# A selective-scan kernel: states in half blocks, sums on TensorE's column halves, residuals on TensorE and ScalarE

## Chip, cores and metric

One Trainium2 chip, one core of it. The metric is the device time of the whole program in microseconds (us); the time before is the median of 3 runs.

## What is computed

64 sequences of 205 rows (128 made by a token mixer out of `x`, 77 of text) and 1024 channels go through an attention-like state-space layer and a feed-forward layer, each with a layer norm ahead and a residual. The part that matters here:

```python
A = -jnp.exp(A_log)                                  # 1024 channels x 16 states
xp = jnp.einsum('bld,rd->blr', x, x_proj_w)          # x is the layer norm of h
dt_in, B, C = xp[..., :32], xp[..., 32:48], xp[..., 48:]
dt = jax.nn.softplus(jnp.einsum('blr,dr->bld', dt_in, dt_proj_w) + dt_proj_b)
dA = jnp.exp(dt[..., None] * A)
dBx = dt[..., None] * B[:, :, None, :] * x[..., None]
def step(h, inp):
    dA_t, dBx_t, C_t = inp
    h = dA_t * h + dBx_t
    y = jnp.einsum('bdn,bn->bd', h, C_t)             # sum over the 16 states
    return (h, y)
y = ys + D * x
h = h + y                                            # first residual
h = h + ffn(layernorm(h))                            # second residual, dequantized weights
```

## The kernel before, in words

Constants, the token mixer and the dequantized weights take the first 480 us or so; `scan_pass` takes the rest. It is a software pipeline over the 64 sequences. In entry `u` the scan of sequence `u` runs, while sequence `u+1` is prepared (layer norm 1, transpose, x and dt projections), `u-1` gets its first residual, layer norm 2 and the feed-forward product, and `u-2` its second residual. Two entries are one body of a hardware loop.

The scan of a sequence has 32 chunks. A chunk is one block of 128 channels (on the partitions) and 4 of the 16 states (205 columns each, 820 in all). For each chunk:

- ScalarE writes `decay = exp(dt * A)` into one of two PSUM buffers, 4 activations of 205 columns (L1003). It waits for the buffer's last reader, two chunks back.
- GpSimd writes `B * u` into one of 8 ring buffers (L1107), where `u = dt * x` was made by it earlier (L1128).
- VectorE scans the 820 columns (L1162). A large dt at column 0 (`reset` on ScalarE, L1085) makes the decay there 0, so that a state does not run into the next.
- The product with `C` is made by VectorE (L1168, chunks in the tuple `ON_DVE`, 19 of 32) or by GpSimd (L1113, the other 13, three chunks later).
- TensorE adds the states up: an identity of 128x128 times each 205-column slice, accumulated in the PSUM bank `y_ps` over 4 chunks (L899), after one product with `diag(D)` (L893). It stands `LAG` = 3 chunks behind. ScalarE copies the block out (`blk`, L1041).

All other work stands in tables written out by hand, one per engine: `PE_PLAN`, `ACT_PLAN`, `DVE_PLAN` and `POOL_PLAN` say behind which chunk each stage stands. Both residuals come as TensorE transposes into one of two exchange banks (`xch`, L915 and L946) that VectorE adds to the rows in `h1` (`add`, L1183; `finish`, L1197), 8 additions a sequence. `mean` for layer norm 2 then reads the 1024 columns again with an accumulator (L1019). The exchange banks go round in the order of `X_ORDER`. SyncE issues all transfers in program order in its `entry`: keep the rows, load the next, spread B and C over 128 partitions (`spread`, L840 and L842), write the result, load the rows for the residual.

```python
for n in range(CN):
    last = nc.tensor.matmul(y_ps, ident[:, :], ring[:, c % RING, n * LEN:(n + 1) * LEN],
                            start=False, stop=(c % 4 == 3 and n == CN - 1))
last.then_inc(sum_done, 1)
```

## Time and profile before

| | |
|---|---|
| median of 3 runs | 6199.3 us (6199.27 to 6200.41) |
| the profiled execution, its own time | 6200.29 us |
| its span | 6198.4 us |
| TensorE's granted clock, mean | 0.979 |
| busy: PE, DVE, POOL, ACT | 93%, 92%, 92%, 83% of the span |
| sequences | 64, one every 87.5 us |

The span is the time from the first to the last instruction. Busy times are unions: two instructions of an engine that overlap at their edges count once, so a mean duration times a count comes to more than the busy time. Consecutive small instructions of ScalarE and VectorE overlap by some 0.06 to 0.1 us, and the distance from start to start is what one of them really takes of its engine. A float32 product is two passes on TensorE, with two records; a transpose is one.

### The profile page before, as it was taken

Reading aid. Unit: us, or ns where it says so; the run is one execution under the profiler, and the core shown is the slowest. Engines: PE = TensorE matmul, PEld = TensorE weight load, DVE = VectorE, ACT = ScalarE, POOL = GpSimd, SP = SyncE. Lnnn points to the kernel's source line nnn. Section 1 sums busy time; section 2 is a strip of 40 time slices with the busy share of each in tenths; the row PEclk is TensorE's granted clock in tenths of the full one; section 3 lists DMA queues with packets and bytes.
Section 4 is the critical chain, followed back from the end, with each engine's and each line's share of the span. In section 5 each row is a group of like instructions: output and inputs, shape, how many; then the busy total and the mean of one; then the engine's idle time right before and its main releaser. Section 6 shows DMA issues by size and latency. Waiting matters only on the chain. (4 is left out here: it accounts for less than half of the span.)

```text
span 6198.4 us, 111922 instructions
## 1 busy us (share of the span) xinstructions
PE 5792.6 (93%) x35091; PEld 5385.1 (87%) x35091; DVE 5699.7 (92%) x4564; ACT 5122.6 (83%) x12831; POOL 5709.3 (92%) x3484
## 2 busy tenths in 40 slices
PE   4686999999999999999999999999999999999998
PEld 3555899999999999999999999999999999999997
DVE  8766999999999999999999999999999999999996
ACT  5716888888888888888888888888888888888885
POOL 4627999999999999999999999999999999999995
PEclk9887999999999999999999999999999999999999
DMA  4701222122212221222122212221222212221220
GB/s 94 161 2 66 83 88 71 67 83 88 74 64 83 88 78 66 78 88 83 61 78 88 88 56 80 86 88 61 77 83 88 72 67 83 88 78 61 83 83 34
DMA packets 115881, 478.49 MB, mean 77 GB/s; under 512 B 17441, under 2 KB 52401, under 8 KB 107122
## 3 DMA queue, kind: packets, MB, share of 16 engines
q1 hardware_dynamic: 115314, 471.10, 22.2%
q8 instruction: 335, 5.49, 0.4%
q14 instruction: 232, 1.90, 0.1%
HBM read 327.82 MB, written 143.24 MB: 76 GB/s over the span
## 5 line engine op out<-in xcount | busy, mean ns | idle before, releaser
L1107 POOL TENSOR_TENSOR s_ring<-s_bc,s_u_t 128x820 f32<-128x820 f32 x2048 | 3617.5, 1788 | 4.2 <-DMA s_bc<-rows_bc 4.2
L1003 ACT ACTIVATE s_decay<-s_dt_t,a_neg 128x205 f32<-128x205 f32 x8192 | 3047.2, 420 | 418.4 <-DVE s_ring L1168 347.5
L899 PE MATMUL s_y_ps<-s_ring,ident 128*128 128x205 f32 x16384 | 3140.6, 341 | 113.5 <-issue 61.5
L899 PEld LDWEIGHTS s_y_ps<-s_ring,ident 128*128 128x128 f32 x16384 | 2864.1, 191 | 204.9 <-POOL s_ring L1113 112.8
L1162 DVE TENSOR_TENSOR_SCAN s_decay<-s_decay,s_ring 128x820 f32<-128x820 f32 x1216 | 2265.0, 1863 | 193.6 <-ACT s_decay L1003 180.0
L1113 POOL TENSOR_TENSOR s_ring<-s_ring,s_bc 128x820 f32<-128x820 f32 x832 | 1605.4, 1930 | 77.7 <-DVE s_ring L1162 77.6
L1162 DVE TENSOR_TENSOR_SCAN s_ring<-s_decay,s_ring 128x820 f32<-128x820 f32 x832 | 1543.3, 1855 | 40.9 <-ACT s_decay L1003 40.9
L932 PE MATMUL s_xch<-s_x_t,w_low 128*128 128x205 f32 x8192 | 1523.6, 338 | 0.6 <-ACT s_x_t L1046 0.2
L932 PEld LDWEIGHTS s_xch<-s_x_t,w_low 128*128 128x128 f32 x8192 | 1422.0, 190 | 35.4 <-issue 30.6
L1168 DVE TENSOR_TENSOR s_ring<-s_decay,s_bc 128x820 f32<-128x820 f32 x1216 | 1230.2, 1012 | 41.7
L893 PE MATMUL s_y_ps<-s_x_t,s_d_diag 128*128 128x205 f32 x1024 | 279.6, 355 | 35.1 <-ACT s_x_t L1041 35.1
L1046 ACT ACTIVATE s_x_t<-s_xch 128x512 f32<-128x512 f32 (+1 forms) x512 | 244.5, 502 | 66.0 <-PE s_xch L923 64.4
L1128 POOL TENSOR_TENSOR s_u_t<-s_dt_t,s_x_t 128x410 f32<-128x410 f32 x256 | 271.7, 1061 | 18.1 <-DVE s_dt_t L1190 18.1
L1060 ACT ACTIVATE s_y_t<-s_xch,y_bias 128x205 f32<-128x205 f32 x512 | 213.7, 417 | 89.8 <-PE s_xch L932 89.8
L1041 ACT ACTIVATE s_x_t<-s_y_ps 128x205 f32<-128x205 f32 x512 | 169.6, 331 | 140.9 <-PE s_y_ps L899 140.3
L964 PE MATMUL s_p_ps<-s_xp,dtw_t 33*128 33x205 f32 x1024 | 248.2, 363 | 7.6 <-DVE s_dt_t L1190 7.1
L437 PE MATMUL t_kb<-t_mag,t_gw 128*128 128x256 f32 x512 | 138.8, 431 | 104.5 <-POOL t_gw L319 104.5
L893 PEld LDWEIGHTS s_y_ps<-s_x_t,s_d_diag 128*128 128x128 f32 x1024 | 169.7, 190 | 75.7 <-ACT s_x_t L1041 57.9
L964 PEld LDWEIGHTS s_p_ps<-s_xp,dtw_t 33*128 33x128 f32 x1024 | 166.2, 188 | 66.4 <-issue 56.9
L437 PEld LDWEIGHTS t_kb<-t_mag,t_gw 128*128 128x128 f32 x512 | 106.6, 215 | 127.1 <-POOL t_gw L319 62.6
L1197 DVE TENSOR_TENSOR s_h<-s_xch,s_h 128x512 f32<-128x512 f32 (+1 forms) x256 | 172.6, 675 | 37.6 <-PE s_xch L946 37.6
L955 PE MATMUL s_p_ps<-s_x_t,xpw_t 128*65 128x205 f32 x1024 | 200.8, 339 | 0.6 <-ACT s_x_t L1046 0.6
(165 smaller groups left out, 4224.0 us busy)
## 6 DMA issues: line engine op xcount, KB each, us to landing
s_bc<-rows_bc SPq DMA_DIRECT2D x64, 3280.0 KB, 11.0
mixed<-t_res SPq DMA_DIRECT2D x32, 1024.0 KB, 9.5
s_x_in<-mixed SPq DMA_DIRECT2D x64, 512.0 KB
s_h<-mixed SPq DMA_DIRECT2D x64, 512.0 KB
before<-s_h SPq DMA_DIRECT2D x64, 512.0 KB
out<-s_h SPq DMA_DIRECT2D x64, 512.0 KB
s_x_in<-in_txt SPq DMA_DIRECT2D x64, 308.0 KB
s_h<-in_txt SPq DMA_DIRECT2D x64, 308.0 KB
```

What stands on the lines that cost most here:

```text
L437: last = nc.tensor.matmul(kb[b][:, QL * k:QL * k + QL], gw[:, half, h, 2 * k:2 * k + 2, :], mag[:, half, h * QL:(h + 1) * QL], start=True, ...
L893: nc.tensor.matmul(y_ps, d_diag[:, j, :], x_t[:, par, j, :], start=True, stop=False)
L899: last = nc.tensor.matmul(y_ps, ident[:, :], ring[:, c % RING, n * LEN:(n + 1) * LEN], start=False, stop=(c % 4 == 3 and n == CN - 1))
L932: last = nc.tensor.matmul(bank[:, 0:LEN], t["w_low"][:, i, P * o:P * o + P], x2_t[:, i, :], start=(i == 0), stop=(i == ND - 1))
L964: last = nc.tensor.matmul(p_ps[:, LEN * k:LEN * k + LEN], t["dtw_t"][:, P * j:P * j + P], xp[0:RANK + 1, :], start=True, stop=True)
L1003: last = A.activation(decay[s % 2][:, n * LEN:(n + 1) * LEN], dt_t[:, par, j, :], ACT.Exp, scale=t["a_neg"][:, j, n0 + n:n0 + n + 1])
L1046: A.activation(target[:, 4 * side:4 * side + 4, cols(k)], bank[:, 0:4 * w].rearrange("p (j l) -> p j l", j=4), ACT.Copy).then_inc(empty, 1)
L1107: nc.gpsimd.tensor_tensor(ring[:, s % RING, :].rearrange("p (n l) -> p n l", n=CN), bc[:, par, n0:n0 + CN, :], u_t[:, j, :].unsqueeze(1).b ...
L1113: nc.gpsimd.tensor_tensor(ring[:, c % RING, :], ring[:, c % RING, :], bc[:, par, n0:n0 + CN, :].rearrange("p n l -> p (n l)"), ALU.mult).t ...
L1128: nc.gpsimd.tensor_tensor(u_t[:, 2 * r:2 * r + 2, :], dt_t[:, par, 2 * r:2 * r + 2, :], x_t[:, par, 2 * r:2 * r + 2, :], ALU.mult).then_in ...
L1162: V.tensor_tensor_scan(out=decay[s % 2] if s in ON_DVE else ring[:, s % RING, :], data0=decay[s % 2], data1=ring[:, s % RING, :], initial= ...
L1168: V.tensor_tensor(ring[:, s % RING, :], decay[s % 2], bc[:, par, n0:n0 + CN, :].rearrange("p n l -> p (n l)"), ALU.mult).then_inc(dve_hc, 1)
```

## The change

- **Half blocks.** A chunk now is one half block of 64 channels and 8 of the 16 states: partitions 0 to 63 hold the even states, 64 to 127 the odd ones. Chunks are as large and as many as before. dt and u are made in the old layout (`dt_n`, `u_n`) and transferred into the new one (`dt_t`, `u_t`) by SyncE, 4 transfers of 64 partitions for each pair of blocks and each of the two, 32 a sequence. The transfer of dt leaves column 0 out, where a large value was set once; `reset` goes. B and C are spread as two transfers of 64 partitions with half the states each.
- **Sums.** TensorE sums two chunks at a time, at every even chunk, `SUM_LAG` = 4 behind. The weights are `stack`, two identities of 64x64 on top of each other (128x64), which add the two partition halves; the products of the even chunk go to partitions 0 to 63 of `y_ps`, those of the odd chunk to 64 to 127, alternating. As many products as before, each with half the output width; `diag(D)` takes two instead of one.
- **Residuals.** TensorE also adds the rows: identity times `h1` (512 columns) opens each exchange bank, and the four transposes become products that accumulate on it. ScalarE copies the bank to `h1`, for the first residual with an accumulator, so that `mean` of layer norm 2 is two operations on one column. VectorE's 8 additions go.
- **C products.** `ON_DVE` holds 22 chunks instead of 19; GpSimd has 10 instead of 13.
- **Order.** All plans and `X_ORDER` are new, and SyncE's entry follows `SP_ORDER`, in which the rows of the next sequence are loaded ahead of the second to fourth part of dt and of the kept rows.

```diff
-PE_PLAN = {1: [("ffn_late", 4)], 2: [("add", 0), ("add", 1)], 6: [("add", 2), ("ffn_late", 5)], 7: [("out_low", 0)],
+PE_PLAN = {1: [("ffn_late", 4)], 3: [("add", 0), ("out_low", 0)], 4: [("add", 1), ("add", 2)], 5: [("add", 3)],
+           6: [("ffn_late", 5)], 7: [("ffn_late", 6)], 9: [("turn1", 0)], 10: [("turn1", 1)], 11: [("ffn_late", 7)],
...
-ACT_PLAN = {0: [("mean1", 0)], 1: [("mean1", 1)], 3: [("ffn_late", 4), ("blk", -1)], 4: [("var1", 0)], 5: [("var1", 1)],
+ACT_PLAN = {0: [("mean1", 0)], 1: [("mean1", 1)], 2: [("ffn_late", 4), ("blk", -1)], 3: [("var1", 0)],
+            4: [("var1", 1), ("add", 0)], 5: [("out_low", 0)], 6: [("add", 1), ("add", 2)], 7: [("norm1", 0)],
+            8: [("mean2", 0)], 9: [("add", 3), ("ffn_late", 5), ("blk", 0)], 10: [("var2", 0)],
...
+DVE_PLAN = {19: [("dt", 0)], 24: [("dt", 1)], 27: [("dt", 2)], 31: [("dt", 3)]}
+POOL_PLAN = {5: [("root1", 0)], 9: [("u_hi", 2)], 14: [("u_hi", 3)], 17: [("root2", 0)], 22: [("u_lo", 0)], 28: [("u_lo", 1)]}
...
+SP_ORDER = [("u_hi", 2), ("u_hi", 3), ("load", 0), ("steps", 0), ("u_lo", 0), ("spread", 0), ("write", 0), ("load_rows", 0),
+            ("steps", 1), ("steps", 2), ("keep", 0), ("steps", 3), ("u_lo", 1)]
...
-ON_DVE = (1, 3, 4, 5, 7, 9, 11, 13, 14, 15, 17, 19, 21, 23, 24, 25, 27, 29, 31)
+ON_DVE = (0, 1, 2, 4, 5, 7, 9, 10, 11, 12, 13, 15, 16, 17, 18, 19, 21, 22, 24, 26, 27, 31)
 EDGE = 512 - 2 * LEN
 LAG = 3
+SINGLE = NB // 2
+SUM_LAG = LAG + 1
+SUM_SLOT = SUM_LAG % 2
...
+def half_block(s):
+    return 2 * (s // 4) + s % 2
...
+        def dt_place(par, b):
+            return b if b < SINGLE else SINGLE + par * (NB - SINGLE) + b - SINGLE
...
-                sp.dma_start(bc[:, par, :, :], rows_bc[par:par + 1, :, :].broadcast_to([P, 2 * NS, LEN])).then_inc(bc_in[par], 16)
+                for i in range(2):
+                    sp.dma_start(bc[64 * i:64 * i + 64, par, :, :],
+                                 rows_bc[par:par + 1, i::2, :].broadcast_to([64, 2 * NK, LEN])).then_inc(bc_in[par], 16)
+            def halves(target, place, source, r, first, signal):
+                for i in range(2):
+                    for h in range(2):
+                        sp.dma_start(target[64 * i:64 * i + 64, place + h:place + 4:2, first:],
+                                     source[64 * h:64 * h + 64, 2 * r:2 * r + 2, first:]).then_inc(signal, 16)
+            def steps(v, par, r):
+                wait(sp, p_empty, v * P_USES + r + 2)
+                halves(dt_t, dt_place(par, 4 * r), dt_n, r, 1, dt_in[r])
+            def inputs(v, r):
+                wait(sp, u_done, v * 4 + r + 1)
+                halves(u_t, 4 * r, u_n, r, 0, u_in[r])
...
             def sums(u, par, c):
                 j = c // 4
+                sides = [slice(64 * h, 64 * h + 64) for h in range(2)]
                 if c % 4 == 0:
                     wait(pe, y_done, u * ND + j)
                     if c == 0 and isinstance(u, int) and u == 0:
                         wait(pe, diag_made, ND)
-                    nc.tensor.matmul(y_ps, d_diag[:, j, :], x_t[:, par, j, :], start=True, stop=False)
-                if c in ON_DVE:
-                    wait(pe, dve_hc, u * PER_DVE + by_dve(c))
-                else:
-                    wait(pe, pool_hc, u * PER_POOL + by_pool(c))
+                    for h in range(2):
+                        nc.tensor.matmul(y_ps[sides[h], :], d_diag[:, j, sides[h]], x_t[:, par, j, :], start=True, stop=False)
+                for e in range(2):
+                    if c + e in ON_DVE:
+                        wait(pe, dve_hc, u * PER_DVE + by_dve(c + e))
+                    else:
+                        wait(pe, pool_hc, u * PER_POOL + by_pool(c + e))
                 for n in range(CN):
-                    last = nc.tensor.matmul(y_ps, ident[:, :], ring[:, c % RING, n * LEN:(n + 1) * LEN],
-                                            start=False, stop=(c % 4 == 3 and n == CN - 1))
-                last.then_inc(sum_done, 1)
+                    for h in range(2):
+                        last = nc.tensor.matmul(y_ps[sides[h], :], t["stack"][:, :], ring[:, (c + h) % RING, n * LEN:(n + 1) * LEN],
+                                                start=False, stop=(c % 4 == 2 and n == CN - 1))
+                        if n == CN - 1:
+                            last.then_inc(sum_done, 1)
             def chunk(u, par, s, x, scan, after):
-                if s >= LAG and scan:
-                    sums(u, par, s - LAG)
-                if s < LAG and after:
-                    sums(u - 1, 1 - par, s - LAG + CHUNKS)
+                if s % 2 != SUM_SLOT:
+                    return
+                if s >= SUM_LAG and scan:
+                    sums(u, par, s - SUM_LAG)
+                if s < SUM_LAG and after:
+                    sums(u - 1, 1 - par, s - SUM_LAG + CHUNKS)
...
             def add(v, par, r, x):
                 k, side = r // 2, r % 2
                 bank, full = claim(x, "add", r)
+                if r == 0:
+                    wait(pe, rows_in[par], (v - par) * 16 + 32)
                 wait(pe, y_done, v * ND + ND)
+                nc.tensor.matmul(bank[0:rows(k), :], ident[0:rows(k), 0:rows(k)], h1[0:rows(k), par, k, 512 * side:512 * side + 512],
+                                 start=True, stop=False)
                 for j in range(4):
-                    last = nc.tensor.transpose(bank[0:rows(k), P * j:P * j + P], x_t[:, par, 4 * side + j, cols(k)], ident[:, :])
+                    last = nc.tensor.matmul(bank[0:rows(k), P * j:P * j + P], x_t[:, par, 4 * side + j, cols(k)], ident[:, :], start=False, stop=(j == 3))
                 last.then_inc(full, 1)
...
             def mean(which, v, par, k, x):
                 n = rows(k)
+                minus_mean = t["ln_in"][0:n, which - 1, 0, k:k + 1]
                 if which == 1:
                     wait(act, loaded, v * 32 + 32)
+                    A.activation(xn[0:n, k, :], x_in[0:n, k, :], ACT.Copy, accum_out=ln_sum[0:n, k:k + 1]).then_inc(ln_piece[which], 1)
+                    wait(act, ln_piece[which], v * LN_DONE + PIECE[which]["mean", k, 0])
+                    A.activation(minus_mean, ln_sum[0:n, k:k + 1], ACT.Copy, scale=-1.0 / DIM).then_inc(ln_piece[which], 1)
                 else:
                     for side in (0, 1):
                         b, c = x.use("add", 2 * k + side)
                         wait(act, x_empty[b], c + 1)
-                A.activation(xn[0:n, k, :], rows_to_norm(which, par)[0:n, k, :], ACT.Copy,
-                             accum_out=ln_sum[0:n, which - 1, k:k + 1]).then_inc(ln_piece[which], 1)
-                wait(act, ln_piece[which], v * LN_DONE + PIECE[which]["mean", k, 0])
-                A.activation(t["ln_in"][0:n, which - 1, 0, k:k + 1], ln_sum[0:n, which - 1, k:k + 1], ACT.Copy,
-                             scale=-1.0 / DIM).then_inc(ln_piece[which], 1)
+                    A.activation(minus_mean, half_sum[0:n, k, 0:1], ACT.Copy, scale=-1.0 / DIM).then_inc(ln_piece[which], 1)
+                    wait(act, ln_piece[which], v * LN_DONE + PIECE[which]["mean", k, 0])
+                    A.activation(minus_mean, half_sum[0:n, k, 1:2], ACT.Identity, scale=-1.0 / DIM, bias=minus_mean).then_inc(ln_piece[which], 1)
...
+            def add(v, par, r, x):
+                k, side = r // 2, r % 2
+                bank, empty = take(x, "add", r)
+                A.activation(h1[0:rows(k), par, k, 512 * side:512 * side + 512], bank[0:rows(k), :], ACT.Copy,
+                             accum_out=half_sum[0:rows(k), k, side:side + 1]).then_inc(empty, 1)
+            def finish(name, v, par, k, x):
+                side = ("out_low", "out_high").index(name)
+                bank, empty = take(x, name, k)
+                if side == 0 and k == 0:
+                    wait(act, kept[par], (v - par) * 16 + 32)
+                A.activation(h1[0:rows(k), par, k, 512 * side:512 * side + 512], bank[0:rows(k), :], ACT.Copy).then_inc(empty, 1)
...
-            def reset(v, par, side):
-                wait(act, u_done, v * 4 + 2 * side + 2)
-                d = dt_t[:, par, 4 * side:4 * side + 4, 0]
-                A.activation(d, d, ACT.Identity, bias=large[:, 0, :]).then_inc(reset_done, 1)
...
             def inputs(u, par, s):
-                j, n0 = s // 4, CN * (s % 4)
+                b, k0 = half_block(s), CN * (s // 2 % 2)
                 if s == 0:
-                    wait(pool, bc_in[par], (u - par) * 8 + 16)
+                    wait(pool, bc_in[par], (u - par) * 16 + 32)
                 if s % 8 == 0:
-                    wait(pool, u_done, u * 4 + s // 8 + 1)
+                    wait(pool, u_in[s // 8], u * 64 + 64)
                 wait(pool, sum_done, u * CHUNKS + s - (RING - 1))
-                nc.gpsimd.tensor_tensor(ring[:, s % RING, :].rearrange("p (n l) -> p n l", n=CN), bc[:, par, n0:n0 + CN, :],
-                                        u_t[:, j, :].unsqueeze(1).broadcast_to([P, CN, LEN]), ALU.mult).then_inc(dbx_done, 1)
+                nc.gpsimd.tensor_tensor(ring[:, s % RING, :].rearrange("p (n l) -> p n l", n=CN), bc[:, par, k0:k0 + CN, :],
+                                        u_t[:, b, :].unsqueeze(1).broadcast_to([P, CN, LEN]), ALU.mult).then_inc(dbx_done, 1)
...
-            def add(v, par, r, x):
-                k, side = r // 2, r % 2
-                bank, empty = take(x, "add", r)
-                if r == 0:
-                    wait(dve, rows_in[par], (v - par) * 16 + 32)
-                V.tensor_tensor(h1[0:rows(k), par, k, 512 * side:512 * side + 512], bank[0:rows(k), :],
-                                h1[0:rows(k), par, k, 512 * side:512 * side + 512], ALU.add).then_inc(empty, 1)
```

**TensorE** in the second entry of the loop body, around the first residual (`s_y_ps` is the bank of sums, `s_xch` an exchange bank). Before:

```order
197 L899 MATMUL s_y_ps<-s_ring,ident 128x205 x4
...
199 L915 MATMUL s_xch<-ident,s_x_t 128x128 x4
...
201 L915 MATMUL s_xch<-ident,s_x_t 128x128 x4
...
203 L893 MATMUL s_y_ps<-s_x_t,s_d_diag 128x205
...
205 L899 MATMUL s_y_ps<-s_ring,ident 128x205 x4
...
207 L899 MATMUL s_y_ps<-s_ring,ident 128x205 x4
...
209 L899 MATMUL s_y_ps<-s_ring,ident 128x205 x4
...
211 L899 MATMUL s_y_ps<-s_ring,ident 128x205 x4
212 L915 MATMUL s_xch<-ident,s_x_t 77x128 x4
```

And now:

```order
304 L959 MATMUL s_y_ps<-s_ring,stack 64x205 x8
...
306 L980 MATMUL s_xch<-s_h,ident 128x512
307 L983 MATMUL s_xch<-ident,s_x_t 128x128 x4
...
309 L1013 MATMUL s_xch<-s_h,ident 128x512
310 L1016 MATMUL s_xch<-ident,s_y_t 128x128 x4
...
312 L951 MATMUL s_y_ps<-s_x_t,s_d_diag 64x205 x2
...
315 L959 MATMUL s_y_ps<-s_ring,stack 64x205 x8
316 L980 MATMUL s_xch<-s_h,ident 128x512
317 L983 MATMUL s_xch<-ident,s_x_t 128x128 x4
...
319 L980 MATMUL s_xch<-s_h,ident 77x512
```

Groups of 4 products of 128 output rows, each ahead of some other work, have become groups of 8 of 64 output rows; the first residual's transposes follow a product of 512 columns with `s_h`.

**ScalarE** after the changed kernel's chunks 3 to 6 of an entry (`s_decay` is the decay of the next chunk). Now:

```order
404 L1107 ACTIVATE s_xn,s_ln_square<-s_x_in,ln_in 77x1024
...
407 L1115 ACTIVATE s_h,s_half_sum<-s_xch 128x512
...
409 L1074 ACTIVATE s_decay<-s_dt_t,a_neg 128x205 x4
...
412 L1123 ACTIVATE s_h<-s_xch 128x512
...
414 L1074 ACTIVATE s_decay<-s_dt_t,a_neg 128x205 x4
415 L1115 ACTIVATE s_h,s_half_sum<-s_xch 128x512
...
417 L1115 ACTIVATE s_h,s_half_sum<-s_xch 77x512
...
419 L1074 ACTIVATE s_decay<-s_dt_t,a_neg 128x205 x4
```

Three moves of the first residual and one of the second stand between the decays of chunks 5, 6 and 7, where the table before has none of them.

**SyncE**, one entry of the loop body. Before:

```order
99 L824 DMA before<-s_h 128x1024
...
101 L824 DMA before<-s_h 77x1024
...
104 L809 DMA s_x_in<-mixed 128x1024
...
106 L810 DMA s_x_in<-in_txt 77x1024
...
108 L840 DMA rows_bc<-s_xp 32x205
...
110 L842 DMA s_bc<-rows_bc 128x6560
...
112 L824 DMA out<-s_h 128x1024
113 L824 DMA out<-s_h 77x1024
...
115 L809 DMA s_h<-mixed 128x1024
...
117 L810 DMA s_h<-in_txt 77x1024
```

And now:

```order
134 L878 DMA s_u_t<-s_u_n 64x2x205 x4
...
137 L837 DMA s_x_in<-mixed 128x1024
...
141 L878 DMA s_dt_t<-s_dt_n 64x2x204 x4
...
143 L878 DMA s_u_t<-s_u_n 64x2x205 x4
...
147 L871 DMA s_bc<-rows_bc 64x16x205 x2
...
149 L852 DMA out<-s_h 128x1024
...
152 L837 DMA s_h<-mixed 128x1024
...
156 L878 DMA s_dt_t<-s_dt_n 64x2x204 x4
...
158 L878 DMA s_dt_t<-s_dt_n 64x2x204 x4
...
161 L852 DMA before<-s_h 128x1024
...
165 L878 DMA s_dt_t<-s_dt_n 64x2x204 x4
...
167 L878 DMA s_u_t<-s_u_n 64x2x205 x4
```

The load of `s_h` stands ahead of three of the four groups of `s_dt_t`, and `before<-s_h` behind it instead of first.

## Rows read from the trace of the kernel before

**Rows 1.** Stretches: start and end, length; busy time (and count) by engine; clock, DMA share, GB/s.

```profile
100.00:200.00 100.00, 69.14 (x606) 55.30 (x604) 89.89 (x111) 82.69 (x136) 61.69 (x27) 0.86 0.72 157
420.00:424.00 4.00, 4.00 (x84) 2.16 (x76) 3.19 (x2) 0.00 (x0) 2.90 (x1) 1.00 0.02 4
3000.00:4000.00 1000.00, 971.74 (x5630) 914.98 (x5631) 947.62 (x717) 868.46 (x2214) 977.22 (x602) 0.99 0.22 80
```

**Rows 2.** One instruction a sequence, L1065: duration in ns, first and last start.

```profile
L1065 ACT ACTIVATE s_xp<-s_p_ps,xp_one x64: 407/428/430, 490.4 to 6004.1; 65x205 f32<-65x205 f32 x64
```

**Rows 3.** Waits of 3000 to 4000 us: who for whom, us, times, longest.

```profile
DVE s_decay L1162 <- ACT s_decay L1003: 32.0, 36, 1.8
ACT s_x_t L1041 <- PE s_y_ps L899: 23.6, 32, 1.1
...
DVE s_ring L1162 <- ACT s_decay L1003: 8.5, 6, 1.6
```

**Rows 4.** VectorE in order of time: start us, duration us, line, operation.

```profile
3000.30 1.85 DVE L1162 TENSOR_TENSOR_SCAN s_ring<-s_decay,s_ring 128x820 f32<-128x820 f32 x1
3002.08 1.85 DVE L1162 TENSOR_TENSOR_SCAN s_decay<-s_decay,s_ring 128x820 f32<-128x820 f32 x1
...
3004.89 1.87 DVE L1162 TENSOR_TENSOR_SCAN s_decay<-s_decay,s_ring 128x820 f32<-128x820 f32 x1
...
3078.29 0.68 DVE L1197 TENSOR_TENSOR s_h<-s_xch,s_h 128x512 f32<-128x512 f32 x1
3078.89 1.86 DVE L1162 TENSOR_TENSOR_SCAN s_ring<-s_decay,s_ring 128x820 f32<-128x820 f32 x1
...
3087.99 1.87 DVE L1162 TENSOR_TENSOR_SCAN s_decay<-s_decay,s_ring 128x820 f32<-128x820 f32 x1 [1.78 <-ACT s_decay L1003]
```

**Rows 5.** GpSimd in order of time.

```profile
3003.39 1.94 POOL L1113 TENSOR_TENSOR s_ring<-s_ring,s_bc 128x820 f32<-128x820 f32 x1
3005.27 1.80 POOL L1107 TENSOR_TENSOR s_ring<-s_bc,s_u_t 128x820 f32<-128x820 f32 x1
```

**Rows 6.** ScalarE in order of time.

```profile
3019.44 0.59 ACT L1046 ACTIVATE s_x_t<-s_xch 128x512 f32<-128x512 f32 x1
3019.92 0.54 ACT L1077 ACTIVATE s_dt_t<-s_dt_t 128x410 f32<-128x410 f32 x1
...
3072.66 1.05 ACT L1019 ACTIVATE s_xn<-s_h 128x1024 f32<-128x1024 f32 x1
3073.61 0.19 ACT L1019 ACTIVATION_READ_ACCUMULATOR s_xn<-s_h 128x1 f32 x1
3073.83 0.20 ACT L1022 ACTIVATE ln_in<-s_ln_sum 128x1 f32<-128x1 f32 x1
```

**Rows 7.** TensorE's weight loads in order of time, one for each pass.

```profile
3010.89 2.80 PEld L899 LDWEIGHTS s_y_ps<-s_ring,ident 128*128 128x128 f32 x16
...
3014.18 1.35 PEld L899 LDWEIGHTS s_y_ps<-s_ring,ident 128*128 128x128 f32 x8
3015.77 0.64 PEld L964 LDWEIGHTS s_p_ps<-s_xp,dtw_t 33*128 33x128 f32 x4 [0.25 <-issue]
3016.66 0.30 PEld L893 LDWEIGHTS s_y_ps<-s_x_t,s_d_diag 128*128 128x128 f32 x2 [0.25 <-issue]
...
3065.24 0.86 PEld L915 LDWEIGHTS s_xch<-ident,s_x_t 128*128 128x128 f32 x8 [0.75 <-ACT s_x_t L1041]
```

**Rows 8.** TensorE's products in the dequantization, L607: 64x64 tiles in turn.

```profile
419.43 5.57 PE L607 MATMUL q_w_ps<-q_mask,q_diagonal 64*64 64x512 bf16 x100
```

**Rows 9.** Weight loads of 65 and of 128 columns: ns min/median/max.

```profile
L955 PEld LDWEIGHTS s_p_ps<-s_x_t,xpw_t x1024: 134/137/236, 485.4 to 6003.5; 128*65 128x65 f32 x171
...
L899 PEld LDWEIGHTS s_y_ps<-s_ring,ident x16384: 186/190/338, 512.5 to 6136.1; 128*128 128x128 f32 x200
```

**Rows 10.** DMA issues: size of one in KB and median us to landing.

```profile
s_bc<-rows_bc SPq DMA_DIRECT2D x64, 3280.0 KB, 11.0
mixed<-t_res SPq DMA_DIRECT2D x32, 1024.0 KB, 9.5
```

163 lines of the change are left out of this document (85 added, 78 removed), and 3 rows, old and new, of the table ACT_PLAN.

## The prediction

> **What bounds the kernel now.** First the stretches [rows 1]: from 3000 to 4000 us, in the middle of the 64 scans, GpSimd is busy 977 of 1000 us, TensorE 972, VectorE 948, ScalarE 868; TensorE's granted clock is 0.99, which is the 2.4 GHz level. No engine has room, so what is taken from one helps only if the others give way too. Then the length of an entry: an instruction that comes once a sequence starts first at 490.4 and last at 6004.1 us [rows 2], 63 distances of 87.52 us. 1000 us are 11.43 entries, so an entry holds 85.5 us of GpSimd, 85.0 of TensorE, 82.9 of VectorE and 76.0 of ScalarE. Then the waits [rows 3]: VectorE never waits for GpSimd. It waits for the decay, 32.0 + 8.5 us in the stretch or 3.5 an entry, and ScalarE, late with it, has waited for the sums among others (23.6 us, 2.1 an entry): TensorE waits for GpSimd's products, ScalarE for TensorE, VectorE for ScalarE. So the end is set by a ring of nearly full engines. One wait of 1.78 us [rows 4] stands at the jump back of the two-entry loop, 0.9 an entry, and will stay.
>
> I count per entry, from start to start, and multiply by 63 at the end.
>
> **VectorE.** The scan of a chunk takes 1.78 us from its start to the next, with its own C product 2.81 [rows 4], so three more C products cost 3 x 1.03 = 3.1. An addition of the residual takes 0.60 [rows 4]; eight go: -4.8. Busy 82.9 -> 81.2. VectorE's entry also has 87.5 - 82.9 - 3.5 = 1.1 us that no wait explains, small gaps at its own results, which stay.
>
> **GpSimd.** Three C products of 1.88 us [rows 5] go: -5.6, 85.5 -> 79.9. The inputs to the ring are as large and as many as before.
>
> **ScalarE.** Eight moves of 512 columns out of PSUM at 0.48 [rows 6] are 3.8, four accumulator reads at 0.22 are 0.9. The second layer norm's mean loses its two passes over 1024 columns (0.95 with 0.22 for the read each, 2.3) and gains two small operations of about 0.2 [rows 6]. The two resets go; operations on a single column or four take 0.2 to 0.3, so 0.5. Net +2.3: 76.0 -> 78.3. The only engine that gets more.
>
> **TensorE**, where the change is decided. Sums: 8 x (1 + 16) = 136 products, 272 passes at 2.80 / 16 = 0.175 [rows 7], 47.6 us. Now they are 128 + 16 products, 288 passes, on half of the columns. The trace has no product of 128 rows and 64 columns. Upper bound: halves run one after the other, 0.175 each, 50.4. Lower bound: two at a time, 25.2. The nearest row is the dequantization: 100 passes of 512 columns on four tiles, two row halves by two column halves, in 5.57 us, 0.056 each [rows 8] at granted clock 1.00 [rows 1]. At one column a cycle of 2.4 GHz such a pass lasts 0.213, so four are in flight; if only the row halves overlapped, it would be 0.107. The tiles there read as many bytes per partition and time (two streams of 2 bytes at one column a cycle) as two float32 streams at a column in two cycles. I take 25.2.
>
> Other terms. The rows to be added: 8 products of 512 columns at 512/205 x 2 x 0.175 = 0.87, 7.0 in all. The 32 transposes become products of two passes; a transpose takes 0.86 / 8 = 0.11 [rows 7], so +3.4. And changing the tile shape costs: around the products of 33 rows (L964) the loads stand still 0.25 us twice; 8 passes from 3014.18 would be over at 3015.58 but the next load is at 3015.77, and 4 passes later the next group is at 3016.66 instead of 3016.47 [rows 7]. 0.38 for a change and back. Sums now stand at 16 places of an entry, 15 with other work between: 5.7. Sum: 85.0 - 47.6 + 25.2 + 7.0 + 3.4 + 5.7 = 78.7.
>
> By the Trainium skill it would come out otherwise: "TensorE: Matmul & The Clock Gate", Part 3, says that a weight load overlaps running matmuls only when its row group is another one, and both column halves have the same rows; the sums would cost at least the upper bound of 50.4, TensorE 103.9. Here the trace speaks against the plain form of it: loads of 128 columns last 0.19 [rows 9], and yet 16 passes with the same rows take 0.175 each [rows 7]. A weaker form is a rival below.
>
> **Transfers.** 32 more of 104 KB an entry, 3.35 MB, while B and C fall from 3.28 to 1.64. SyncE spends 0.35 to 0.5 us on issuing one, some 14 of 87 us, between waits that are long. Packets are of 820 bytes, 6144 an entry. The nearest traffic, 1024-byte packets of the token mixer [rows 10], ran at 157 GB/s with 0.72 of the DMA time [rows 1], or 0.075 us a packet and engine: 29 us of the 84 on each of the 16. From 0.22 of the time, less the 11 us of B and C [rows 10], the share goes to 0.4 or 0.45. None of it is on the path as long as it lands in time. The order leaves this: dt's first part goes behind chunk 19's stage and is needed 12 chunks later; u's behind GpSimd's chunks 9, 14, 22 and 28, needed 7 to 12 chunks later; the rows for the residual are issued when the last exchange bank is out (chunk 25) and the write has landed, perhaps chunk 29, and are needed at chunk 3, 6 chunks or 16 us later; the kept rows go out near chunk 30 and must be away at chunk 5. A transfer of 820 KB needs under 11 us, as 3280 KB took 11.0 [rows 10]. I cost the transfers at nothing; without that cover each would be 3 to 5 us of an entry. What dt and u add ahead of the very first scan, two landings, is +3 us once.
>
> **The entry after.** GpSimd 79.9, TensorE 78.7, ScalarE 78.3, VectorE 81.2: VectorE is the fullest. Its floor is 81.2 + 1.1 + 0.9 = 83.2. To that comes decay that is late. ScalarE may be ahead of VectorE by no more than two buffers, about one chunk. In chunks 3 to 6 it now has two variances (about 1.4 each), one residual move of 0.5 and three of 0.7 with the read, 5.4, and four decays at about 1.43, 5.7, together 11.1; VectorE has two chunks of 1.78 and two of 2.81 there, 9.2. Of these 1.9 us, 1.3 (a chunk of 2.81 less a decay) can be worked ahead: 0.6 late, and I give the rest of the entry as much. What was due to waiting for sums goes, since TensorE has 5 us to spare. 83.2 + 1.2 = 84.4. Bounds: 83.2 with no decay late; 86.4 if the 2.6 us of late decay that stand there now stay and half of ScalarE's 2.3 more falls on the path (83.2 + 2.6, and some).
>
> 63 x (87.5 - 84.4) = 195. The profiled execution took 6200.3, 0.9 of a us above the median of 6199.3: 6200.3 - 195 + 3 = 6008, and 6007 beside the median. Bounds of this case: 6199 - 271 + 3 = 5931 and 6199 - 69 + 3 = 6133.
>
> **Rivals.**
>
> *Column halves overlap in part (slower).* If a load can be only one pass ahead of the products, over both halves together, each pair of passes that should run together waits for a load. A load of 65 columns lasts 0.137, one of 128 0.190 [rows 9], so 64 columns are 0.05 of the load's own time: two products of the two halves take 2 x (0.175 + 0.05) = 0.45 in place of 0.35. That is 144 x 0.225 = 32.4 for the sums, TensorE 85.9 of work and the 2.5 idle that it has now: 88.4, 63 x 0.9 = +57 and 3: about 6260. It decides from the point where a product of a half costs over 0.21 us. The rule of the Trainium skill's "TensorE: Matmul & The Clock Gate", Part 3, taken loosely, is a reason for it. Against: the dequantization alternates four tiles with loads between and reaches four in flight, though each of its tiles gets one pass in turn, where here both passes of a float32 product follow each other on the same half.
>
> *The change doesn't do what it says.* The halves run one after the other: TensorE 78.7 + 25.2 = 103.9 and 2.5 idle, 63 x 18.9 = +1190, about 7390. Only the dequantization's row speaks against it, plainly.
>
> *ScalarE sets the entry.* If its 2.3 us more fall wholly on the path, on top of the 3.5 us of today's late decay: 81.2 + 1.1 + 3.5 + 2.3 = 88.1, +0.6, or 6240; half of that is 6170 or so. For: the crowded chunks 3 to 6. Against: it is idle 11.5 us an entry now and would be 6.
>
> *Transfers late.* One part of dt, u or the rows misses its chunk by 3 us in each entry: 87.4, about 6195. For: SyncE takes them in order, each behind the waits of others. Against: 6 chunks or more between.
>
> **How the numbers follow.** Forecast 0.77. Halves in part 0.07, halves in turn 0.03, ScalarE 0.08 (of which 0.03 still faster), transfers 0.05 (0.02 faster, 0.02 the same, 0.01 slower). A measurement of this kernel tells 0.2%, 12 us, from no change. Faster: 0.77 + 0.03 + 0.02 = 0.82. The same: 0.02 + 0.02 of ScalarE's = 0.04. Slower: 0.07 + 0.03 + 0.03 + 0.01 = 0.14. The range is the forecast's own, 5930 to 6135, with some 0.7 of its 0.77 inside and 0.1 from the better parts of ScalarE's and the transfers' cases: 0.8 in all.
>
> **What the profile after would show.** Right: entries of 84 to 85 us between the starts of the copy of `xp`; groups of 16 half passes of the sums from 1.4 to 1.5 us; loads standing still about 0.2 us on either side of them; TensorE busy under 95% of the middle, VectorE 96% or more; VectorE waiting for the decay under 2 us an entry and never for GpSimd; no wait for a DMA by ScalarE, GpSimd or TensorE. Wrong: groups of 16 half passes of 1.8 us (in part) or 2.8 us (in turn); TensorE over 97% with ScalarE waiting for `y_ps`; VectorE waiting for the decay 3 us or more an entry right behind the residual moves; anything waiting for `s_dt_t`, `s_u_t` or `s_h` from a DMA.

## The result, and the profile after

The changed kernel takes 6162.1 us (median of 4 runs, 6159.4 to 6167.4) against 6199.3: ratio 0.9939, interval 0.9927 to 0.9951. It is faster, by 37 us or 0.6%, where 192 were forecast; 6162 lies above the range's upper end of 6135. One execution in all that follows, the profiled one of e12 at 13250 us, was slow and is left out, so e12 has a time and no rows of a trace.

The profiled execution took 6159.4 us with a span of 6157.7. Counted from first scan to first scan, 63 entries now take 5481.2 us instead of 5539.7: **-58.5**, or 0.93 an entry where 3.1 were forecast. The last entry's scans give 2.5 more, the first scan starts 4.7 later, and from the last scan's start to the end of the span it takes 15.5 longer (below): -40.8, and the two executions differ by 40.9.

The stretch from 3000 to 4000 us, to be held against [rows 1] (busy us and count of PE, PEld, DVE, ACT, POOL, then granted clock, DMA share, GB/s):

```profile
3000.00:4000.00 1000.00, 890.72 (x6415) 683.79 (x6410) 931.47 (x666) 893.37 (x2321) 921.21 (x572) 0.98 0.42 101
```

At 87.2 us an entry these are 11.47 entries, so an entry holds 77.7 of TensorE (forecast 78.7), 81.2 of VectorE (81.2), 77.9 of ScalarE (78.3) and 80.3 of GpSimd (79.9), and the DMA share is 0.42 (0.4 to 0.45). Every engine's work was forecast to within 1 us. What came out otherwise is when they stand still. The waits of the same stretch, where [rows 3] had 32.0 + 8.5 us for the decay:

```profile
POOL s_rstd L1221 <- ACT ln_in L1110: 57.4, 11, 8.3
DVE s_decay L1238 <- ACT s_decay L1074: 48.9, 36, 6.0
...
ACT s_decay L1074 <- issue: 35.8, 12, 3.9
...
DVE s_ring L1238 <- ACT s_decay L1074: 8.5, 12, 0.7
```

VectorE's wait for the decay has grown, and its longest is 6.0 us. ScalarE waits 12 times for "issue", for nothing the profile shows: twice in each of the six jumps back of the two-entry loop. VectorE's timeline, the first scan of four entries in a row:

```profile
3036.14 1.87 DVE L1238 TENSOR_TENSOR_SCAN s_decay<-s_decay,s_ring 128x820 f32<-128x820 f32 x1 [5.28 <-ACT s_decay L1074]
...
3120.49 1.86 DVE L1238 TENSOR_TENSOR_SCAN s_decay<-s_decay,s_ring 128x820 f32<-128x820 f32 x1
...
3210.28 1.87 DVE L1238 TENSOR_TENSOR_SCAN s_decay<-s_decay,s_ring 128x820 f32<-128x820 f32 x1 [5.59 <-ACT s_decay L1074]
...
3294.63 1.86 DVE L1238 TENSOR_TENSOR_SCAN s_decay<-s_decay,s_ring 128x820 f32<-128x820 f32 x1
```

The distances are 84.35, 89.79 and 84.35. Over 28 pairs of entries the mean is 84.64 for the entry without a jump at its end and 89.74 for the one with it; before it was 87.69 and 88.29, and VectorE's gap at the jump was 1.4 on the mean. Now it is 5.1. (The gap is the distance from the last scan of an entry to the first of the next, less the same distance where there is no jump.)

What stands at that jump, on TensorE and on ScalarE (timeline: start, busy us, engine, line; in brackets the idle time before and its releaser):

```profile
3031.29 0.57 PE L951 MATMUL s_y_ps<-s_x_t,s_d_diag 128*64 128x205 f32 x4 [3.04 <-issue]
...
3032.47 1.14 ACT L1074 ACTIVATE s_decay<-s_dt_t,a_neg 128x205 f32<-128x205 f32 x3 [3.75 <-issue]
...
3035.67 0.44 ACT L1074 ACTIVATE s_decay<-s_dt_t,a_neg 128x205 f32<-128x205 f32 x1 [2.06 <-issue]
```

The same place in the kernel before:

```profile
3054.34 1.50 ACT L1003 ACTIVATE s_decay<-s_dt_t,a_neg 128x205 f32<-128x205 f32 x4 [2.38 <-issue]
...
3055.91 4.37 PE L899 MATMUL s_y_ps<-s_ring,ident 128*128 128x205 f32 x14 [2.21 <-issue]
```

ScalarE stands still once for 2.4 us before; now 3.8 us, and again 2.1 us after three of the four activations of the first decay. One jump is not the mean. From 600 to 6000 us there are 29 jumps back, first before and then now (waits: us, times, longest):

```profile
ACT s_decay L1003 <- issue: 62.4, 29, 2.4
PE s_y_ps L899 <- issue: 61.5, 29, 2.4
...
ACT s_decay L1074 <- issue: 159.9, 58, 4.7
PE s_y_ps L951 <- issue: 65.3, 29, 3.6
```

A jump back cost ScalarE 2.15 us and costs it 5.5 now, in two stops of 3.6 and 1.9 on the mean; TensorE's stop has hardly changed, 2.12 and 2.25. What has grown is ScalarE's. What else differs there is the DMA traffic, here in windows of 2 us of the changed kernel (columns as in the first fence):

```profile
3028.00:3030.00 2.00, 0.25 (x2) 0.00 (x0) 1.97 (x2) 0.72 (x2) 2.00 (x2) 1.00 1.06 222
3030.00:3032.00 2.00, 0.71 (x8) 0.64 (x10) 0.86 (x2) 0.00 (x0) 2.00 (x2) 1.00 0.86 290
3032.00:3034.00 2.00, 2.00 (x17) 1.22 (x13) 0.00 (x0) 1.14 (x3) 2.00 (x2) 0.66 0.91 281
```

and in windows at a jump of the kernel before:

```profile
3052.00:3054.00 2.00, 1.70 (x10) 1.38 (x8) 1.97 (x3) 0.00 (x0) 2.00 (x2) 1.00 0.05 12
3054.00:3056.00 2.00, 0.09 (x1) 0.09 (x1) 0.45 (x2) 1.66 (x5) 2.00 (x2) 1.00 0.01 4
```

The DMA share is 0.86 to 1.06 now and was 0.01 to 0.05. SyncE's queue shows what moves: parts of dt and the kept rows, for which there is time until chunk 5 or later, are issued right at the jump:

```profile
3022.88 5.29 SPq L878 DMA_DIRECT2D s_dt_t<-s_dt_n  x8
3028.43 1.50 SPq L852 DMA_DIRECT2D before<-s_h  x2
3030.89 3.13 SPq L878 DMA_DIRECT2D s_dt_t<-s_dt_n  x4
```

The page of the changed kernel lists instructions as queues of their own on the same 16 DMA engines (packets, MB, share):

```profile
q1 hardware_dynamic: 535170, 578.26, 39.5%
q8 instruction: 368, 6.03, 0.4%
q14 instruction: 235, 1.93, 0.1%
```

**Theory (J).** At the jump back an engine has to fetch the instructions of the loop's start. That fetch goes through the DMA engines and stands behind the data transfers under way. The Trainium skill, "Runtime: NRT & Kernel Launch", section "Instruction fetch mechanics", says as much of the first half: fetch runs ahead in sequence in blocks of 256 instructions, and a branch taken out of that window has to wait for a DMA. It gives no price, and says nothing of other transfers. Rivals: the jump costs what it costs, and the decay is late because the new order puts more of ScalarE's work ahead of it; or a part of dt lands late.

The traces hold the fetch itself. At each of the 29 jumps of every kernel in this table a packet of q14 starts while ScalarE stands still, and ScalarE goes on after it. ScalarE's first stop behind a jump falls into three pieces, here as means in us over the 29 jumps (the e-runs are explained below):

| run | first stop (least, most) | until the packet starts | the packet | from its end to the first activation | DMA share in the stop |
|---|---|---|---|---|---|
| before | 2.15 (1.99, 2.39) | 0.39 | 0.42 | 1.35 | 0.05 |
| after | 3.60 (2.83, 4.68) | 1.49 | 0.49 | 1.63 | 0.92 |
| e1 | 2.80 (2.27, 3.76) | 0.93 | 0.46 | 1.41 | 0.67 |
| e3 | 10.46 (9.27, 11.43) | 7.35 | 0.46 | 2.65 | 1.14 |
| e5 | 2.46 (2.28, 2.70) | 0.59 | 0.42 | 1.45 | 0.04 |
| e8 | 2.17 (1.99, 2.39) | 0.34 | 0.44 | 1.39 | 0.04 |
| e9 | 2.49 (2.28, 2.68) | 0.57 | 0.46 | 1.46 | 0.04 |
| e13 | 3.51 (2.49, 4.54) | 1.46 | 0.47 | 1.57 | 0.91 |

The packet takes as long as ever, but it starts later when data is in flight. So the fetch does stand behind the data, as theory J says.

Last, TensorE's loads, where the forecast was least sure (to be held against [rows 7]):

```profile
3020.87 0.20 PEld L951 LDWEIGHTS s_y_ps<-s_x_t,s_d_diag 128*64 128x64 f32 x4 [0.25 <-issue]
3021.10 1.36 PEld L959 LDWEIGHTS s_y_ps<-s_ring,stack 128*64 128x64 f32 x16
3022.76 0.64 PEld L1034 LDWEIGHTS s_p_ps<-s_xp,dtw_t 33*128 33x128 f32 x4 [0.30 <-issue]
3023.65 1.24 PEld L959 LDWEIGHTS s_y_ps<-s_ring,stack 128*64 128x64 f32 x16 [0.25 <-issue]
```

16 half passes in 1.36 us, 0.085 each: the halves overlap fully.

### The profile page after: what moved, and what is told of

Read it like the earlier page. It is cut to its first block and busy times, and to the rows that moved or that the text cites. A ratio compares the mean times of both kernels' runs of the same rounds, so it can differ in the third digit from the quotient of the medians.

```text
span 6157.7 us, 122204 instructions
## 1 busy us (share of the span) xinstructions
PE 5321.8 (86%) x39187; PEld 4061.5 (66%) x39187; DVE 5567.6 (90%) x4247; ACT 5232.4 (85%) x13343; POOL 5346.7 (87%) x3292
## 5 line engine op out<-in xcount | busy, mean ns | idle before, releaser
L1238 DVE TENSOR_TENSOR_SCAN s_decay<-s_decay,s_ring 128x820 f32<-128x820 f32 x1408 | 2619.1, 1860 | 268.2 <-ACT s_decay L1074 240.3
L959 PE MATMUL s_y_ps<-s_ring,stack 128*64 128x205 f32 x16384 | 1638.0, 343 | 97.7 <-POOL s_ring L1196 74.0
L959 PEld LDWEIGHTS s_y_ps<-s_ring,stack 128*64 128x64 f32 x16384 | 1145.4, 138 | 437.9 <-POOL s_ring L1196 95.2
L1196 POOL TENSOR_TENSOR s_ring<-s_ring,s_bc 128x820 f32<-128x820 f32 x640 | 1234.0, 1928 | 2.6 <-DVE s_ring L1238 2.3
L1238 DVE TENSOR_TENSOR_SCAN s_ring<-s_decay,s_ring 128x820 f32<-128x820 f32 x640 | 1180.8, 1853 | 44.3 <-ACT s_decay L1074 44.2
L980 PE MATMUL s_xch<-s_h,ident 128*128 128x512 f32 (+1 forms) x512 | 298.4, 666 | 183.6 <-ACT s_x_t L1128 147.2
L1013 PE MATMUL s_xch<-s_h,ident 128*128 128x512 f32 (+1 forms) x512 | 289.1, 648 | 102.7 <-ACT s_x_t L1133 101.3
L983 PEld LDWEIGHTS s_xch<-ident,s_x_t 128*128 128x128 f32 (+1 forms) x2048 | 279.6, 184 | 145.4 <-issue 145.4
L951 PE MATMUL s_y_ps<-s_x_t,s_d_diag 128*64 128x205 f32 x2048 | 297.2, 369 | 81.3 <-issue 65.3
L983 PE MATMUL s_xch<-ident,s_x_t 128*128 128x128 f32 (+1 forms) x2048 | 291.1, 289 | 0.0
L1016 PE MATMUL s_xch<-ident,s_y_t 128*128 128x128 f32 (+1 forms) x2048 | 281.4, 282 | 0.0
```

What stands on the lines that cost most here:

```text
L951: nc.tensor.matmul(y_ps[sides[h], :], d_diag[:, j, sides[h]], x_t[:, par, j, :], start=True, stop=False)
L959: last = nc.tensor.matmul(y_ps[sides[h], :], t["stack"][:, :], ring[:, (c + h) % RING, n * LEN:(n + 1) * LEN], start=False, stop=(c % 4 == ...
L980: nc.tensor.matmul(bank[0:rows(k), :], ident[0:rows(k), 0:rows(k)], h1[0:rows(k), par, k, 512 * side:512 * side + 512], start=True, stop=F ...
L983: last = nc.tensor.matmul(bank[0:rows(k), P * j:P * j + P], x_t[:, par, 4 * side + j, cols(k)], ident[:, :], start=False, stop=(j == 3))
L1013: nc.tensor.matmul(bank[0:rows(k), :], ident[0:rows(k), 0:rows(k)], h1[0:rows(k), par, k, 512 * side:512 * side + 512], start=True, stop=F ...
L1016: last = nc.tensor.matmul(bank[0:rows(k), P * j:P * j + P], y_t[:, 4 * side + j, cols(k)], ident[:, :], start=False, stop=(j == 3))
```

## Experiments

"Two entries" is the mean distance from the first scan of one entry to that of the second after it, over 28 pairs; the gap is VectorE's at the jumps among them (28 of them with two entries in a body, 14 with four, 2 with twenty). All ratios are to the kernel before, of 6196 to 6199 us beside these runs.

| run | time, us | ratio, interval | two entries | gap |
|---|---|---|---|---|
| before | 6199.3 | | 175.98 | 1.4 |
| after | 6162.1 | 0.9939 (0.9927 to 0.9951) | 174.38 | 5.1 |
| e1 | 6153.7 | 0.9932 (0.9915 to 0.9948) | 174.03 | 3.9 |
| e2 | 6147.3 | 0.9921 (0.9900 to 0.9942) | 173.67 | 4.0 |
| e3 | 6460.2 | 1.0416 (1.0398 to 1.0434) | 185.17 | 9.7 |
| e4 | 6115.4 | 0.9862 (0.9845 to 0.9878) | 172.90 | 6.2 |
| e5 | 6108.7 | 0.9862 (0.9846 to 0.9879) | 172.44 | 2.8 |
| e6 | 6462.7 | 1.0430 (1.0412 to 1.0447) | 183.87 | 4.8 |
| e7 | 6387.1 | 1.0305 (1.0287 to 1.0322) | 181.05 | 4.0 |
| e8 | 6196.8 | 0.9998 (0.9988 to 1.0008) | 175.80 | 1.4 |
| e9 | 6060.7 | 0.9780 (0.9767 to 0.9793) | 170.78 | 2.0 |
| e10 | 6055.1 | 0.9771 (0.9758 to 0.9784) | 170.70 | 2.8 |
| e11 | 6142.8 | 0.9913 (0.9898 to 0.9928) | 174.02 | 1.9 |
| e12 | 6150.4 | 0.9922 (0.9907 to 0.9937) | | |
| e13 | 6120.8 | 0.9874 (0.9858 to 0.9891) | 172.80 | 3.0 |
| e14 | 6064.4 | 0.9783 (0.9766 to 0.9799) | 170.93 | 2.0 |

**e3 and e8: the same extra transfers, at the jump or in the middle.** Both are the kernel before, with four stores of 840 KB of weights to a scratch tensor in each entry, behind chunk 30 (e3) or chunk 14 (e8). Nothing waits for them but the stores of the next entry. e8 has 14 for 30 below, and issues them ahead of `spread`.

```diff
+            def extra(u):
...
+                wait(sp, extra_done, u * (16 * 4))
+                wait(sp, scan_done, u * CHUNKS + 30)
+                for k in range(4):
+                    sp.dma_start(scratch[k:k + 1, :, :, :].rearrange("a p j l -> (a p) j l"), t["w_low"][:, :, 0:LEN]).then_inc(extra_done, 16)
```

> The kernel before with four more transfers of 840 KB in 820-byte packets, weights to a scratch tensor, issued in every entry behind chunk 30, so that they are in flight at the jump; nothing waits for them. Theory J: the excess of the entry with the jump rises from 0.6 us to 3 to 6 us, the time from 6199 by 60 to 160 us to about 6310. Rival B: the excess stays 0.6, the time at 6199 to 6215.

> The kernel before with the same four extra transfers of 840 KB an entry, but issued behind chunk 14, far from the jump. Theory J: nothing waits for instructions there, the time stays at 6199 to 6230 us, and the gap at the jump at 1.4 us. Rival C (data traffic slows the engines' own accesses or the other transfers, wherever it is): as with the transfers at the jump, 6350 to 6460 us.

The same bytes cost 263 us at the jump (60 to 160 were expected) and nothing in the middle. ScalarE in e3, at a jump:

```profile
3169.32 1.50 ACT L1014 ACTIVATE s_decay<-s_dt_t,a_neg 128x205 f32<-128x205 f32 x4 [10.39 <-issue]
```

and the windows ahead of it, in which from 3166 to 3168 no compute engine works at all while the DMA share is over 1:

```profile
3164.00:3166.00 2.00, 0.00 (x0) 0.00 (x0) 0.00 (x0) 0.00 (x0) 0.03 (x1) 0.74 1.02 232
3166.00:3168.00 2.00, 0.00 (x0) 0.00 (x0) 0.00 (x0) 0.00 (x0) 0.00 (x0) 0.50 1.19 174
```

In e8 the stop at the jump is the old one:

```profile
3053.88 1.50 ACT L1014 ACTIVATE s_decay<-s_dt_t,a_neg 128x205 f32<-128x205 f32 x4 [2.32 <-issue]
```

That is theory J in a kernel with no late dt and no new order on ScalarE: the fetch's packet waits 7.35 us for its start in e3 and 0.34 in e8. The granted clock falls to 0.50, the 1.2 GHz level, once TensorE has stood still; the jump takes that too.

**e1 and e12: dt and u hardly moved.** The transfers of dt and u move 2 columns (e1), or 2 columns of 16 partitions (e12), in place of 204 and 205. The scan then computes on a constant 0.5, so only the times count.

```diff
-                        sp.dma_start(target[64 * i:64 * i + 64, place + h:place + 4:2, first:],
-                                     source[64 * h:64 * h + 64, 2 * r:2 * r + 2, first:]).then_inc(signal, 16)
+                        sp.dma_start(target[64 * i:64 * i + 64, place + h:place + 4:2, 1:3],
+                                     source[64 * h:64 * h + 64, 2 * r:2 * r + 2, 1:3]).then_inc(signal, 16)
...
+            nc.gpsimd.memset(u_t[:, :, :], 0.5)
+            nc.gpsimd.memset(dt_t[:, :, 1:], 0.5)
```

> The changed kernel with its 32 transfers of dt and u an entry cut to 2 columns each (dt and u are constants, so the scan computes on other numbers): same instructions, same waits, 3.3 MB an entry less to move. Theory J (the jump back of the loop costs 5.1 us more in an entry with a jump than in one without, because the instructions fetched there queue behind data that is in flight): the excess falls from 5.1 us to 1 to 2.5 us (the rows and the kept rows are still moving), the time from 6162 to 6030 to 6100 us. Rival B (the jump costs more because the bodies are longer or more engines meet there empty, whatever the DMA does): the excess stays near 5, the time within 10 us of 6162.

> The changed kernel, in its own order, with the transfers of dt and u cut to 16 packets of 8 bytes each instead of 128 of 820 (dt and u are constants). With 2 columns and all 128 packets the gap at the jump only fell from 5.1 to 3.9 us. If it is the number of packets in the way of the instruction loads and not the bytes, the gap falls now to 2.8 (kept rows and residual rows still move) or less, the time to 6060 to 6110. If neither matters, it stays 3.9 and 6150.

For e1 6030 to 6100 us was expected, and only 8 us come back; e12 gives 12, the 6150 of its second case, so the number of packets isn't what counts. Both intervals overlap the changed kernel's. The rival that wanted the gap to stay near 5 missed too, for in e1 it goes from 5.1 to 3.9. The waits of e1 from 600 to 6000 us:

```profile
ACT s_decay L1074 <- issue: 126.6, 58, 3.8
PE s_y_ps L951 <- issue: 26.8, 29, 1.3
```

A jump costs ScalarE 4.4 us where it was 5.5, and TensorE 0.9 where it was 2.25. So the bytes of dt and u do lengthen the stops. They were most of the traffic there: in the 2.5 us around the start of the stop, packets of 816 bytes (dt) take 0.83 of the DMA engines' time in the changed kernel, and the kept rows' packets of 4096 bytes 0.13; in e1 the latter take 0.34. But the time hardly follows: the entry with the jump is 1.0 us shorter (88.77), the one without it 0.6 us longer (85.25). Why, no run shows; e10 below has the same in a plainer form.

It also speaks against the rival of a late part of dt: with 8 bytes a packet the stops are still there, and they are ScalarE's for issue, not for `s_dt_t`.

**e2 and e5: transfers moved off the jump.** e2 puts `keep` first in `SP_ORDER`. e5 does so too, moves the second part of u ahead of dt's third and fourth, and holds all parts of dt but the first until the next entry's first decay is written, that is, until ScalarE is past the jump.

```diff
-SP_ORDER = [("u_hi", 2), ("u_hi", 3), ("load", 0), ("steps", 0), ("u_lo", 0), ("spread", 0), ("write", 0), ("load_rows", 0),
-            ("steps", 1), ("steps", 2), ("keep", 0), ("steps", 3), ("u_lo", 1)]
+SP_ORDER = [("keep", 0), ("u_hi", 2), ("u_hi", 3), ("load", 0), ("steps", 0), ("u_lo", 0), ("spread", 0), ("write", 0), ("load_rows", 0),
+            ("steps", 1), ("u_lo", 1), ("steps", 2), ("steps", 3)]
...
                 wait(sp, p_empty, v * P_USES + r + 2)
+                if r == 1:
+                    wait(sp, decay_done, v * CHUNKS + 1)
```

> The changed kernel with the kept rows saved first in SyncE's entry, as before the change, instead of eleventh, right at the jump: 820 KB less in flight there, the same bytes in all. Theory J: the excess of the entry with the jump falls from 5.1 to 3 to 4 us, the time by 30 to 60 us to about 6115. Rival B: no change, 6155 to 6170. Theory T (transfers of dt late for ScalarE): no change, since the parts of dt go out when they did.

> The changed kernel with the kept rows saved first and the second to fourth part of dt and the second of u held back until ScalarE has made the first decay behind the jump: the same transfers, but only the rows for the residual still run ahead of the jump. Theory J (instruction loads behind the jump queue behind data): VectorE's gap at the jump falls from 5.1 us to 1.4 to 2.5, the time to 6040 to 6090 us. Rival B (longer bodies): the gap stays 4 or more, over 6130. A third way: the parts held back come late for chunk 8, then a gap opens there.

e2 gives 15 us, where 30 to 60 were expected; its runs spread from 6135 to 6159 and its interval holds the changed kernel's ratio, so its time shows nothing, though the gap fell to 4.0. e5 gives 53 us, clear of noise, but less than expected (a gap of 2.8 for 1.4 to 2.5, 6109 us for 6040 to 6090). Nothing is computed otherwise; only the time of issue differs. Which of the transfers that e5 moves matters most no run shows. The jump on ScalarE in e5:

```profile
3010.87 1.14 ACT L1076 ACTIVATE s_decay<-s_dt_t,a_neg 128x205 f32<-128x205 f32 x3 [2.39 <-issue]
3012.90 0.44 ACT L1076 ACTIVATE s_decay<-s_dt_t,a_neg 128x205 f32<-128x205 f32 x1 [0.89 <-issue]
```

and two windows there:

```profile
3008.00:3010.00 2.00, 1.03 (x11) 0.60 (x12) 1.97 (x2) 0.48 (x2) 2.00 (x2) 1.00 0.05 12
3010.00:3012.00 2.00, 2.00 (x19) 1.57 (x16) 0.62 (x2) 1.13 (x3) 2.00 (x2) 1.00 0.02 4
```

The first stop is 2.46 on the mean of 29 jumps, near the 2.15 before the change, at a DMA share of 0.04; what makes the last 0.3 stays open. A second one of 0.77 stays, three activations on (0.89 in the line above).

**e9 and e13: the second stop.** Eight activations of one column stand ahead of ScalarE's loop and shift all that follows in its instruction stream; e9 on top of e5, e13 on the changed kernel.

```diff
+            for k in range(8):
+                A.activation(padding[:, k:k + 1], t["eps_ln"][:, :], ACT.Copy)
```

> The kernel of the quiet jump with eight one-column activations ahead of ScalarE's loop, which only shift the address of its loop body. In the quiet-jump kernel ScalarE stops twice at the jump, 2.39 us ahead of the first decay and 0.89 in the middle of it. If the second stop is the edge of the block of instructions that was fetched, three instructions behind the jump's target, it goes or moves: VectorE's gap falls from 2.8 to about 1.9 us, the time from 6109 to 6075 to 6090. If it has to do with the third decay itself or the data, both stay as they are.

> The changed kernel with eight activations of one column ahead of ScalarE's loop and nothing else: the place of its jump target in the instruction stream moves, the transfers stay at the jump. If two things add up (the fetch's first part queued behind the loads, the second part at an edge three instructions behind the target), then one stop of ScalarE's two at the jump goes, the other stays at 3 to 4 us: VectorE's gap at the jump 3.5 to 4.5 in place of 5.1, 20 to 50 us less than the changed kernel, 6110 to 6145. If the quiet was all and the edge costs only what is left of it, no change: 6155 to 6165. If the edge was all, a gap of 2 and 6060.

The second stop is gone in both, at all 29 jumps. ScalarE at a jump of e9:

```profile
3157.03 1.50 ACT L1079 ACTIVATE s_decay<-s_dt_t,a_neg 128x205 f32<-128x205 f32 x4 [2.39 <-issue]
```

and of e13:

```profile
3187.39 1.50 ACT L1077 ACTIVATE s_decay<-s_dt_t,a_neg 128x205 f32<-128x205 f32 x4 [3.40 <-issue]
```

The shift alone gives 41 us, the quiet jump alone 53, both 101: they add up (94 expected from the two). e9 came out better than expected (6061 us for 6075 to 6090), e13's time as expected and its gap of 3.0 below the 3.5 that it should have kept. So there are two causes, and both are the fetch. The first part stands behind the transfers (first stop 3.5 against 2.5 us, e13 and e9). The second is an edge three activations behind the jump's target, where the next part has to be fetched as well. The page of e9, and that of e13, has

```profile
q14 instruction: 206, 1.69, 0.1%
```

where the changed kernel and e5 have 235 packets: 29 fewer, one for each jump back, while q8 keeps its 368. Since only ScalarE's code was shifted, these are its packets. Around each jump there are three of them with the edge and two without, as in the kernel before. And the second stop waits for a packet of its own: it starts 1.33 us (after) or 0.41 us (e5) behind the first activation, lasts 0.4, and ScalarE goes on 1.3 or 1.1 us after its end. The Trainium skill's blocks of 256 instructions (the section named above) are of 16 KB by its own figure. The packets of q8 are of 16 KB too, those of q14 of 8 KB, where the measurement decides.

**e4, e10, e11 and e14: fewer jumps.** 4 or 20 entries in one body in place of 2: the changed kernel (e4), e5 (e10), the kernel before (e11) and e9 (e14).

```diff
-            with engine.Fori(0, (BATCH - 4) // 2) as i:
-                entry(i * 2 + 3, 1, Exchange(i * (2 * X_STEP) + x_start(3)), X_GROUPS)
-                entry(i * 2 + 4, 0, Exchange(i * (2 * X_STEP) + x_start(4)), X_GROUPS)
+            with engine.Fori(0, (BATCH - 4) // 20) as i:
+                for k in range(20):
+                    entry(i * 20 + 3 + k, (3 + k) % 2, Exchange(i * (20 * X_STEP) + x_start(3 + k)), X_GROUPS)
...
```

> The changed kernel with four entries in the body of the loop instead of two: 15 jumps instead of 30, everything else the same. Theory J and rival B both give 15 x 5.1 = 77 us less, 6085 us. If what costs 5 us in every second entry is not the jump but the parity of the buffers, the time stays at 6162.

> The kernel of the quiet jump with 20 entries in the body, 3 jumps instead of 30. If the jump is what is left, each entry takes the 84.5 us of those without one: 27 x 3.5 = 94 us less, 6015. If long bodies cost otherwise (instructions fetched in a row arrive late too, with the data in the way), the entries lengthen and the time is 6040 or more.

> The kernel before with 20 entries in the body. Its entry with the jump is only 0.6 us longer than the other, so 27 x 0.6 = 16 us less: 6183. If the 1.4 us gap at the jump was wholly on the path: 6161.

> The quiet jump and the eight activations ahead of the loop, with four entries in a body. Theory: three entries of 84.7 and one of 86.5 (gap 2.0 at the jump), 63 of them 5365 us against 5379 with two a body: 6045. Rival: what long bodies gave back with twenty entries (entries of 85.3, small gaps at chunks 18 and 26) comes from the length of the body, then the entries are 85.2 and the time stays at 6060 to 6070.

In e4 the entries at three places of the body take 84.8 to 85.1 on the mean and those at the fourth 91.0: the stop belongs to the jump, not to a chunk. It was to take 6085 us and took 6115, for its gap at a jump is 6.2 instead of 5.1. e11 prices the jump in the kernel before. It took 6143 where 6161 or more was expected: two entries take 1.96 us less, and 26 of 28 jumps are gone, so 2.1 a jump. VectorE shows as much there, though not in one piece:

```profile
3055.87 1.86 DVE L1162 TENSOR_TENSOR_SCAN s_ring<-s_decay,s_ring 128x820 f32<-128x820 f32 x1 [1.55 <-ACT s_decay L1003]
3058.58 1.87 DVE L1162 TENSOR_TENSOR_SCAN s_decay<-s_decay,s_ring 128x820 f32<-128x820 f32 x1 [0.85 <-ACT s_decay L1003]
```

The waits before the first two scans behind a jump are 1.3 and 0.85 on the mean.

e10 missed: 6015 was expected and it took 6055. Its entries aren't all half a us longer than those of e5 (84.5). In the middle of a body they alternate, 84.1 and 86.55, and the long ones have two waits that the short ones lack, at chunks 19 and 27 (counted from 0):

```profile
1335.94 1.87 DVE L1242 TENSOR_TENSOR_SCAN s_decay<-s_decay,s_ring 128x820 f32<-128x820 f32 x1 [1.44 <-ACT s_decay L1078]
1357.58 1.87 DVE L1242 TENSOR_TENSOR_SCAN s_decay<-s_decay,s_ring 128x820 f32<-128x820 f32 x1 [1.17 <-ACT s_decay L1078]
```

Ahead of the first, ScalarE has waited 1.56 us for TensorE's dt product (L1038), in the short entry 0.44. Two entries without any jump so take 170.65, and e9's two with one take 170.78: a stop of 2.5 us costs the changed kernel next to nothing, because the entry behind it takes 84.5 and as a rule has neither wait. That fits e10, and e14, which was to take 6045 and took 6064, gaining nothing on e9. What holds the long bodies back is late decay in entries far from a jump; what starts the alternation stays open.

**e6: the halves one after the other.** The loops over `n` and `h` in `sums` are swapped, so that eight passes of a half stand in a row.

```diff
-for n in range(CN):
-    for h in range(2):
+for h in range(2):
+    for n in range(CN):
```

> The changed kernel with the two loops of the sums swapped: all four products of the even chunk, then all four of the odd one, so that the two column halves hardly run together. If the halves overlap only when they alternate, a group of 16 passes takes 2.6 us instead of 1.36, TensorE has 22 us more an entry, 99 to 102, and sets the end: about 7100 us. If the half-wide products are cheaper by themselves, or the sums are not near the path, the time stays near 6162.

TensorE's loads in e6:

```profile
3006.50 1.99 PEld L959 LDWEIGHTS s_y_ps<-s_ring,stack 128*64 128x64 f32 x16 [0.16 <-issue]
3015.31 2.11 PEld L959 LDWEIGHTS s_y_ps<-s_ring,stack 128*64 128x64 f32 x16
```

The group takes 1.99 to 2.11 us instead of 1.36, and TensorE is busy 966 of 1000 us: the alternation is what lets the halves overlap, and without it the changed kernel is 264 us slower than the kernel before. 7100 was expected, from 2.6 us a group. The loads of 878 such groups show why it is less: on one half they start 0.175 us apart, as the full-width ones did, so a half pass is no cheaper by itself; but the second half's first three run beside the first half's last three. With the halves alternating, two loads start within 0.007 us of each other and the next two 0.17 later.

**e7: 19 C products on VectorE**, as before the change, 13 on GpSimd.

```diff
-ON_DVE = (0, 1, 2, 4, 5, 7, 9, 10, 11, 12, 13, 15, 16, 17, 18, 19, 21, 22, 24, 26, 27, 31)
+ON_DVE = (0, 1, 2, 4, 5, 7, 9, 10, 11, 13, 15, 16, 17, 19, 21, 22, 24, 27, 31)
```

> The changed kernel with 19 C products on VectorE instead of 22 (chunks 12, 18 and 26 go back to GpSimd). If VectorE sets the entries without a jump (84.6 us), it is freed of 3.1 us but GpSimd rises from 79.9 to 85.5 and with its waits sets 87 to 88: 6250 to 6350 us. If late decays set them (ScalarE), fewer products on VectorE change little on that side and GpSimd still decides: the same. If GpSimd has more room than I think, the time falls below 6150.

From the waits of e7 from 3000 to 4000 us:

```profile
PEld s_y_ps L959 <- POOL s_ring L1196: 33.3, 16, 3.3
```

Two entries take 181.05 and the time is 6387, a little over the 6250 to 6350 expected. GpSimd is busy 949 of 1000 us, the most of the four, and TensorE now waits for its products, up to 3.3 us. In this order of work the three more products on VectorE are needed. That GpSimd sets the entry is the likely reading; VectorE's own waits are still for the decay.

## Why the prediction was wrong

- **VectorE, GpSimd, ScalarE, TensorE busy** (81.2, 79.9, 78.3, 78.7): right, measured 81.2, 80.3, 77.9, 77.7.
- **TensorE's sums** at the lower bound of 25.2: right, 288 x 0.085 = 24.5. The rule of the Trainium skill's "TensorE: Matmul & The Clock Gate", Part 3, that a load needs another row group to overlap, would give at least 50.4 by the prediction's estimate; the measurement decides against it here. By e6 it depends on whether neighbouring passes are on different column halves. The rows and the transposes came as priced, 0.86 and 0.89 us in the timeline of TensorE behind the last scan:

```profile
6081.66 1.02 PE L980 MATMUL s_xch<-s_h,ident 128*128 128x512 f32 x2
6082.52 1.05 PE L983 MATMUL s_xch<-ident,s_x_t 128*128 128x128 f32 x8
6083.41 1.02 PE L980 MATMUL s_xch<-s_h,ident 77*77 77x512 f32 x2
```

- **The change of tile shape** at 0.38 there and back: not measured by itself, and the sum of TensorE's work bears it out to within 1 us; the loads stand still 0.25 and 0.30 around a group, where it was 0.25 and 0.25. The Trainium skill's "TensorEngine Tiling (Array Packing)" says that a change of tiling mode drains the engine; these standstills fit it.
- **"One wait of 1.78 us stands at the jump back of the two-entry loop, 0.9 an entry, and will stay"**: this is the step that failed, together with **"I cost the transfers at nothing"**. The reading was wrong to begin with: the wait of 1.78 us in [rows 4], at 3087.99, is at chunk 11 of an entry. The jump is at 3055.87, with the two waits shown at e11. The term came out near (2.1 a jump, 1.1 an entry), by luck. I took the stop at the jump for a constant and asked of the transfers only whether their data would land in time. They did. But the new order puts transfers at the jump (3.35 MB of dt and u an entry are new, 1.7 MB net), and ScalarE's fetch stands behind them; and the new code put an edge three activations behind the jump's target. VectorE's gap went from 1.4 to 5.1 us. e3, e8 and e5 show the first cause, e9 and e13 the second.
- **The size of it.** By scans an entry of before is 87.93, 0.4 more than by the first copy of `xp` [rows 2], whose first instance stands ahead of the loop; the forecast of 84.4 is 84.8 on that basis, 169.6 for two, 83.9 for one without its half of the jump. Measured: 84.64 without a jump (+0.7) and 89.74 with it, where 83.9 + 1.8 = 85.7 was forecast (+4.0). With both causes taken away e9's two entries take 170.8, and e9 101 us less: so much of the 155 us that the forecast was short is the jump's. But the 84.64 are no entry without a jump's influence: by e10 such entries take 85.3 on the mean, 1.4 over the 83.9.
- **Late decay** of 1.2 us an entry: right in kind, half the size. VectorE waited 48.9 + 8.5 us for the decay from 3000 to 4000 us, some 30 of them at the six jumps; the rest is 2.4 an entry. It waits 0.5 to 1.0 us at chunk 5 and at chunk 7 or 10 (that at 10 for GpSimd), as forecast for chunks 3 to 6, and then, where nothing was forecast by place, 0.7 at chunk 30 and now and then 1.2 at chunk 27 and 1.4 at chunk 19. This second mis-sized term is the likely cause of most of what e9 doesn't give back: 1.2 for two entries (170.8 against 169.6), 38 of 54 us.
- **"+3 once"**: the first scan is 4.7 later, and the drain behind the last scan, which was left out of the forecast, is 15.5 longer. Its last scan starts at 6126.75 of a span of 6198.4 before, and now at 6070.5 of 6157.7. There the banks of both residuals go to and fro between TensorE and ScalarE, which idles in between (timeline of ScalarE):

```profile
6083.61 0.60 ACT L1115 ACTIVATE s_h<-s_xch 128x512 f32<-128x512 f32 x1 [1.16 <-PE s_xch L983]
...
6104.73 0.59 ACT L1123 ACTIVATE s_h<-s_xch 77x512 f32<-77x512 f32 x1 [3.20 <-PE s_xch L1016]
```

That this is its whole cause was not tried.
- **Rivals.** Halves in part or in turn, ScalarE, late transfers: none came. From 600 to 6000 us no engine waits for a DMA. The rival that did come was not among them, though the trace showed its ground: a stop for "issue" on two engines at once, at a place where the DMA share was 0.05.

## What to carry to other kernels

A stop for "issue" at a loop's jump was a DMA read of instructions here: before adding or moving transfers, look at what is in flight there, and keep the few us around the jump free, for instance by waiting with what isn't urgent for a semaphore that an engine raises behind the jump. Where a second stop stands a few instructions behind the target, shift the code ahead of the loop. Read a stop as a mean over all jumps: at single ones it ran from 2.8 to 4.7 us in one trace. And price a stop by a run without it, not by its length. The version to keep is the changed kernel with both, 6061 us in place of 6162, or the quiet order with 20 entries in a body, 6055; the two differ by less than their runs do.

## What the runs showed of the hardware that was not expected

- The jump's stop grows with the traffic at it: ScalarE's first stop is 2.0 to 2.7 us at a DMA share of 0.05 or less (before, e5, e8, e9), 2.5 to 4.7 at 0.7 to 1.0 (after, e13), and 9.3 to 11.4 with four stores of 840 KB queued ahead (e3). What grows is above all the time until the fetch's packet starts, 0.3 to 0.6, 1.5 and 7.4 us on the mean, and not the packet, 0.4 to 0.5.
- A jump's price isn't the gap before the first scan: in the kernel before 2.1 us against 1.4 (e11), with 0.85 more before the second scan; and next to nothing in e9, whose entries without a jump have late decay in its place (e10).
- Eight tiny activations ahead of a loop, run once, made a kernel 41 to 48 us faster.
- Passes of float32 products with the same rows and two column halves run two at a time when they alternate (0.085 us each). In a row on one half they take 0.175 each, as much as a full-width pass, and two groups in a row overlap only where the half changes (0.13 each over 16).
- 3.4 MB an entry more of DMA traffic in mid-entry, on top of a share of 0.22, costs VectorE, ScalarE, GpSimd and TensorE nothing that can be measured (e8: 0.9998, 0.9988 to 1.0008).
